# Feeding x to the attention block: split in SBUF and turned by DMA, loaded ahead of Wv, with the opening's slots rearranged

## What is computed

```python
x = x + xattn(_layernorm(x), ctx, Wq, Wk, Wv, Wo)   # 32 heads of 128, 4 key/value groups
x = x + ffn(_layernorm(x), w_gate, w_up, w_down)    # 512 -> 1376 -> 512, quantised weights and activations
# in xattn: keys and values come from concatenate([context, latents]); latents = _layernorm(x)
```

## Time and profile before

| | |
|---|---|
| median of 3 runs | 822.93 us (822.24 to 824.15) |
| the profiled execution's own time | 823.92 us |
| its span in the trace | 822.1 us |
| PE busy | 780.0 us (95%) |
| DVE, ACT, POOL busy | 599.8, 433.7, 229.4 us |

### The profile page before, as it was taken

The page is one execution under the profiler, slowest core; times in us unless marked ns, Lnnn a source line. Parts: engine busy times, 40 slices in busy tenths (PEclk is TensorE's granted clock), DMA queues, the critical chain, the costliest instruction groups (busy, mean ns, idle before and its releaser), DMA issues.

```text
span 822.1 us, 12689 instructions
## 1 busy us (share of the span) xinstructions
PE 780.0 (95%) x4803; PEld 471.6 (57%) x4803; DVE 599.8 (73%) x1117; ACT 433.7 (53%) x940; POOL 229.4 (28%) x366
## 2 busy tenths in 40 slices
PE   8999999999999999999999999998989999941998
PEld 3456576667666666666666666665544444420445
DVE  5876557788767878768778777888767559989431
ACT  6255446655656655656655655555631019782920
POOL 0120314356343355442456433434300000000000
PEclk9999999999999999999999999999999999985999
DMA  9214046757455666455765546888752000000011
GB/s 318 79 61 145 14 90 143 158 137 141 112 120 131 164 154 134 111 129 115 180 137 137 125 102 131 170 164 151 153 98 47 1 1 0 1 0 0 27 39 39
DMA packets 203582, 85.51 MB, mean 104 GB/s; under 512 B 170369, under 2 KB 187009, under 8 KB 203521
## 3 DMA queue, kind: packets, MB, share of 16 engines
q1 hardware_dynamic: 203520, 84.69, 44.8%
HBM read 31.72 MB, written 10.75 MB: 52 GB/s over the span
## 4 chain that ended last, share of the span: by engine, by line
PE 84%; DVE 9%; DMA 3%; POOL 1%; issue 1%; ACT 1%; SPq 1%; DVEq 0%; ACTq 0%; POOLq 0%
PE bank L328 25%; PE bank L446 12%; PE bank L513 12%; PE bank L430 10%; PE bank L418 10%; PE bank L582 7%; PE bank L450 6%; DMA arena<-in_x 2%; DVE arena L769 2%; DMA arena<-arena 1%; DVE stats L1122 1%; DVE arena L1112 1%; POOL arena L1155 1%; DVE bn L924 1%; PE bank L355 1%
## 5 line engine op out<-in xcount | busy, mean ns | idle before, releaser
L328 PE MATMUL bank<-arena 128*128 128x256 f16 (+1 forms) x1872 | 260.6, 292 | 1.7 <-DVE arena L769 1.7
L328 PEld LDWEIGHTS bank<-arena 128*128 128x128 f16 x1872 | 183.0, 98 | 83.2 <-DVE arena L769 3.2
L1155 POOL TENSOR_SCALAR arena<-arena,rsum 128x256 f32<-128x256 f32 x256 | 133.2, 520 | 299.9 <-DVE rsum L835 285.7
L769 DVE SCALAR_TENSOR_TENSOR arena<-bank,arena 128x512 f16<-128x512 f32 x168 | 114.7, 689 | 121.0 <-ACT arena L590 120.8
L590 ACT ACTIVATE arena<-bank 128x512 f16<-128x512 f32 x168 | 98.8, 597 | 179.2 <-PE bank L430 103.1
L769 DVE SCALAR_TENSOR_TENSOR arena<-arena 128x512 f16<-128x512 f32 (+5 forms) x197 | 171.0, 881 | 17.8 <-ACT arena L590 17.2
L590 ACT ACTIVATE arena<-arena 128x512 f16<-128x512 f32 (+5 forms) x164 | 130.1, 819 | 34.5 <-POOL arena L1185 13.1
L632 ACT ACTIVATE arena<-bank,nmax 128x256 f32<-128x256 f32 x256 | 117.7, 471 | 49.0 <-DVE nmax L827 48.7
L446 PE MATMUL bank<-arena 128*128 128x512 f16 x512 | 121.0, 379 | 0.4 <-ACT arena L590 0.4
L513 PE MATMUL bank<-arena 128*128 128x512 f16 x507 | 109.8, 379 | 0.2 <-DVE stats L1053 0.2
L430 PE MATMUL bank<-arena 128*128 128x512 f16 x384 | 94.6, 383 | 4.1 <-DMA arena<-arena 4.1
(11 more groups left out here) (102 smaller groups left out, 496.2 us busy)
## 6 DMA issues: line engine op xcount, KB each, us to landing
arena<-in_w_units SPq DMA_DIRECT2D x33, 256.0 KB, 3.6
w_ready<-arena SPq DMA_DIRECT2D x33, 256.0 KB, 3.3
arena<-in_wq SPq DMA_DIRECT2D x32, 256.0 KB, 3.6
arena<-in_wo SPq DMA_DIRECT2D x32, 256.0 KB, 3.6
arena<-in_x SPq DMA_DIRECT2D x1, 2048.0 KB, 15.2
out<-arena SPq DMA_DIRECT2D x7, 256.0 KB, 2.0
arena<-in_wk SPq DMA_DIRECT2D x4, 256.0 KB, 5.0
arena<-in_ctx_t SPq DMA_DIRECT2D x4, 256.0 KB, 5.2
```

The costliest lines, as they stand in the source:

```text
L328: last = nc.tensor.matmul(bank, a(i, c), b(j, c), start=start and c == 0 and n == 0, stop=stop and c == chunks - 1 and n == 2)
L769: return nc.vector.scalar_tensor_tensor(out=dst, in0=src, scalar=scale, in1=part, op0=ALU.mult, op1=ALU.subtract)
L1155: done = nc.gpsimd.tensor_scalar(p_s[:, t % 2, :, hh, :], p_s[:, t % 2, :, hh, :], rsum[:, t % 2, hh:hh + 1], P_SCALE, ALU.mult, ALU.mult)
```

## The change

x is loaded in two halves, ahead of Wv. The normalised x carries the factor 64 (folded into `veps`), its upper part is written by ACT (`x_upper`, 128 x 512 a batch), its lower part by POOL (a `tensor_tensor` subtraction of 128 x 512 a batch), both into `x_16` in SBUF, and SP turns each batch with one DMA transpose of 128 x 1024 fp16 into `src_t[:, 5]` (`turn_x`). PE's fp32 transposes and the two splits from their banks are gone. DVE takes two `bn_stats` in each of slots 0 to 3, aggregates in slot 3 and splits Wv there; ACT splits Wv's upper part in slot 3. `ln_apply` stands in slots 5 and 6. The second half of the context is split in two pieces of two chunks, and PE multiplies by pairs. The units of the opening begin in slots 8, 11, 15, 25. At slot 16 ACT waits until all eight transposes have landed, because the buffer of `x_16` becomes that of the split Wq.

```diff
-SLOT_OF = (5, 9, 13, 25)
+SLOT_OF = (8, 11, 15, 25)
+        x_16 = f16(96, 8192).rearrange("p (b r n) -> p b r n", b=B, r=2)
 # SP
+            for half in range(2):
+                sp.dma_start(y[:, 4 * half:4 * half + 4, :], x_d[:, 4 * half:4 * half + 4, :]).then_inc(x_loaded[half], 16)
             sp.dma_start(wkv_raw[:, 1], wv_d).then_inc(wv_loaded, 16)
-            sp.dma_start(y, x_d).then_inc(x_loaded, 16)
+            def turn_x(b):
+                sp.wait_ge(x_lo, b + 1)
+                sp.dma_start_transpose(src_t[:, 5, :, :, b * P:(b + 1) * P].rearrange("p r c t -> p (r c) t"),
+                                       x_16[:, b].rearrange("p r n -> p (r n)")).then_inc(x_turned_in[b // 4], 16)
...
             load_unit(0)
+            for b in range(B):
+                turn_x(b)
             for slot in range(32):
 # PE
-            pe.wait_ge(src_lo, HC + 1)
             for g in range(NG):
-                three(banks[4 + g][:, :], lambda r, c: wkv_s[:, 0, r, c, g * D:(g + 1) * D],
-                      lambda r, c: src_t[:, 0, r, c, 512:TOK], HC).then_inc(kv_mm, 1)
+                for pair in range(2):
+                    pe.wait_ge(src_lo, HC + 1 + pair)
+                    mm = three(banks[4 + g][:, :], lambda r, c: wkv_s[:, 0, r, 2 * pair + c, g * D:(g + 1) * D],
+                               lambda r, c: src_t[:, 0, r, 2 * pair + c, 512:TOK], HC // 2, start=pair == 0, stop=pair == 1)
+                mm.then_inc(kv_mm, 1)
             for b in range(B):
                 v_tile(0, (4 if b < 4 else 8) + b + 1, b, b % 4)
-                if b >= 4:
-                    transpose_x(2 * (b - 4))
-                    transpose_x(2 * (b - 4) + 1)
             for i in range(2):
-                pe.wait_ge(xt_free, i * 4 + 8)
+                pe.wait_ge(x_turned_in[i], 64)
 # ACT
-            hi(src_t[:, 0, 0, :, 512:TOK], ctx_raw[:, :, 512:TOK], X_SCALE).then_inc(src_hi, 1)
-            act.wait_ge(wv_loaded, 16)
-            hi(wkv_s[:, 1, 0], wkv_raw[:, 1], W_SCALE).then_inc(wv_hi, 1)
+            for c in range(0, HC, 2):
+                hi(src_t[:, 0, 0, c:c + 2, 512:TOK], ctx_raw[:, c:c + 2, 512:TOK], X_SCALE).then_inc(src_hi, 1)
...
                     k_hi(slot + 1, 0, slot // 4, slot % 4, slot)
+                    if slot == 3:
+                        act.wait_ge(wv_loaded, 16)
+                        hi(wkv_s[:, 1, 0], wkv_raw[:, 1], W_SCALE).then_inc(wv_hi, 1)
+                    if slot == 7:
+                        for b in range(4):
+                            x_upper(b)
                 elif slot < 16:
+                    if slot < 10:
+                        x_upper(2 * slot - 12)
+                        x_upper(2 * slot - 11)
                     v_hi(slot + 1, (slot - 8) * P, slot % 4)
...
                     if slot == 16:
-                        act.wait_ge(wv_lo, 1)
+                        for turned in x_turned_in:
+                            act.wait_ge(turned, 64)
 # DVE
                     k_lo(slot + 1, 0, slot // 4, slot % 4, slot)
+                    if slot < 4:
+                        dve.wait_ge(x_loaded[slot // 2], 16)
+                        nc.vector.bn_stats(bn[:, 2 * slot, :], y[:, 2 * slot, :]).then_inc(ln_stat, 1)
+                        nc.vector.bn_stats(bn[:, 2 * slot + 1, :], y[:, 2 * slot + 1, :]).then_inc(ln_stat, 1)
+                    if slot == 3:
...
+                        nc.vector.tensor_scalar(veps[:, :], mv[:, :, 1], 1e-5, X_SCALE ** -2, ALU.add, ALU.mult).then_inc(ln_var, 1)
+                        dve.wait_ge(wv_hi, 1)
+                        lo(wkv_s[:, 1, 1], wkv_raw[:, 1], wkv_s[:, 1, 0], W_SCALE).then_inc(wv_lo, 1)
+                    if slot == 5:
+                        dve.wait_ge(ln_rstd, 1)
+                    if 5 <= slot < 7:
+                        for b in range(4):
+                            ln_apply(4 * (slot - 5) + b)
 # POOL
-                if slot == 8:
+                if slot == 4:
                     pool.wait_ge(mhalf_set, 1)
                     pool.wait_ge(ln_var, 1)
                     nc.gpsimd.tensor_tensor(rstd[:, :], veps[:, :], mhalf[:, :], ALU.pow).then_inc(ln_rstd, 1)
+                if slot == 8:
+                    for b in range(B):
+                        pool.wait_ge(x_hi, b + 1)
+                        nc.gpsimd.tensor_tensor(x_16[:, b, 1, :], xln[:, b, :], x_16[:, b, 0, :], ALU.subtract).then_inc(x_lo, 1)
```

More of the change, by code:

```diff
@@ L177, in build @@
         wk_loaded = [sem(f"wk_loaded{c}") for c in range(HC)]
-        wv_loaded, x_loaded = sem("wv_loaded"), sem("x_loaded")
+        wv_loaded, x_loaded = sem("wv_loaded"), [sem("x_loaded0"), sem("x_loaded1")]
         wq_loaded = [sem("wq_loaded0"), sem("wq_loaded1")]
@@ L188, in build @@
         kv_mm, kv_hi, kv_free = sem("kv_mm"), sem("kv_hi"), sem("kv_free")
-        xt_mm, xt_hi, xt_free = sem("xt_mm"), sem("xt_hi"), sem("xt_free")
+        x_hi, x_lo, x_turned_in = sem("x_hi"), sem("x_lo"), [sem("x_turned_in0"), sem("x_turned_in1")]
         ln_stat, ln_mv = sem("ln_stat"), sem("ln_mv")
@@ L342, in v_tile @@
                       lambda r, c: wkv_s[:, 1, r, c, :], HC).then_inc(kv_mm, 1)
[L344 to L350, removed]
             def keep_warm(n):
@@ L369, in _ @@
                         mm.then_inc(kv_mm, 1)
-            pe.wait_ge(src_lo, HC + 1)
             for g in range(NG):
-                three(banks[4 + g][:, :], lambda r, c: wkv_s[:, 0, r, c, g * D:(g + 1) * D],
-                      lambda r, c: src_t[:, 0, r, c, 512:TOK], HC).then_inc(kv_mm, 1)
+                for pair in range(2):
[3 more added lines that the diff above has]
+                mm.then_inc(kv_mm, 1)
             pe.wait_ge(wv_lo, 1)
-            pe.wait_ge(ident_set, 2)
             for b in range(B):
                 v_tile(0, (4 if b < 4 else 8) + b + 1, b, b % 4)
-                if b >= 4:
-                    transpose_x(2 * (b - 4))
-                    transpose_x(2 * (b - 4) + 1)
             for i in range(2):
-                pe.wait_ge(xt_free, i * 4 + 8)
+                pe.wait_ge(x_turned_in[i], 64)
                 for g in range(NG):
@@ L454, in transpose_x2 @@
             def transpose_x2(b):
+                if b == 0:
+                    pe.wait_ge(ident_set, 2)
                 pe.wait_ge(ln2_out, b + 1)
@@ L467, in x_value_tile @@
                       lambda r, c: wkv_s[:, 1, r, c, :], HC).then_inc(kv_mm, 1)
-            pe.wait_ge(xt_free, 12)
             for f in range(3):
@@ L613, in v_hi, with x_upper @@
                 hi(kv[:, 1:5, 2, col:col + P], banks[bank][:, :].rearrange("p (g d) -> p g d", g=NG), PROJ_OUT).then_inc(kv_hi, 1)
[L615 to L618, removed]
+            def x_upper(b):
+                if b == 0:
+                    act.wait_ge(wv_lo, 1)
+                act.wait_ge(ln_out, b + 1)
+                hi(x_16[:, b, 0, :], xln[:, b, :], 1.0).then_inc(x_hi, 1)
             def q_upper(f):
@@ L664, in _ @@
                     k_hi(slot + 1, 0, slot // 4, slot % 4, slot)
+                    if slot == 3:
[4 more added lines that the diff above has]
+                            x_upper(b)
                 elif slot < 16:
+                    if slot < 10:
+                        x_upper(2 * slot - 12)
+                        x_upper(2 * slot - 11)
                     v_hi(slot + 1, (slot - 8) * P, slot % 4)
-                    if slot >= 12:
-                        xt_upper(2 * (slot - 12))
-                        xt_upper(2 * (slot - 12) + 1)
                 elif slot < 24:
                     if slot == 16:
-                        act.wait_ge(wv_lo, 1)
+                        for turned in x_turned_in:
+                            act.wait_ge(turned, 64)
                     k_hi(slot + 1, 1, (slot - 16) // 4, slot % 4, slot % 4)
@@ L781, in _ @@
             dve.sem_inc(kv_free, 4)
-            dve.sem_inc(xt_free, 4)
             dve.sem_inc(g_free, 3)
@@ L796, in v_lo @@
                    kv[:, 1:5, 2, col:col + P], PROJ_OUT).then_inc(kv_free, 1)
[L798 to L802, removed]
             def wq_lower(n):
@@ L896, in _, with ln_apply @@
                 lo(src_t[:, 0, 1, c, 0:512], ctx_raw[:, c, 0:512], src_t[:, 0, 0, c, 0:512], X_SCALE).then_inc(src_lo, 1)
[L897 to L900, removed]
-            for slot in range(32):
-                if slot == 8:
[L904 to L912, removed]
+            for c in range(0, HC, 2):
+                dve.wait_ge(src_hi, HC + 1 + c // 2)
+                lo(src_t[:, 0, 1, c:c + 2, 512:TOK], ctx_raw[:, c:c + 2, 512:TOK], src_t[:, 0, 0, c:c + 2, 512:TOK], X_SCALE).then_inc(src_lo, 1)
+            def ln_apply(b):
+                nc.vector.tensor_scalar(xln[:, b, :], y[:, b, :], mv[:, b, 0:1], rstd[:, b:b + 1],
+                                        ALU.subtract, ALU.mult).then_inc(ln_out, 1)
+            for slot in range(32):
                 if slot == 24:
@@ L921, in _ @@
```

(13 more changed lines are left out.)

## The result

The changed kernel takes 817.0 us (median of 4 runs, 816.17 to 817.2) against 823.39 (4 runs, 822.24 to 824.15): a ratio of 0.992, 95% interval 0.9908 to 0.9933, or 6.4 us won. The forecast was 817.8, from a gain of 5.1. Of all executions behind this document two were disturbed (1201.59 us of before and 2277.39 us of a variant) and are in no ratio. The first page part and the windows of the kernel after answer to the earlier trace rows; two windows at the loop's end are added.

The account below looks back on a forecast made before the run. PE bounds the kernel, busy 780.0 of 822.1 us. Removing waits of 0.54 and 1.09 and transposes of 3.51 wins 5.14, so 822.93 - 5.1 = 817.8 us; range 816.9 to 821.2.

Parts of the forecast that it names:

- The opening: PE before x's key tiles: waits of 0.54 and 1.09 and transposes of 3.51 go, together 5.14 us; start at 47.7.
- rival 2: Opening: DVE and POOL hold each other up, costing PE 0 to 0.9 us; gain about 4.2, time 818.7; chance 0.20.
- Context pieces and Wv: Opening: DVE's context pieces end at 15.1 and 16.2, Wv's split at 26.4; PE asks for Wv at 26.90, margin 0.5.
- POOL's power "ends by 26": Opening, ahead of x's normalisation: POOL's power, 1.70 us in the profile, ends by 26, behind Wv's split.
- the 4 us of cover: Fifth value tile: first `v_lo` done by 33.1, PE wants it at 37.3, so the wait of 1.09 goes.
- The rule on the port: Opening: DVE and GpSimd share one port pair, so normalisations (4 x 1.05 = 4.2) and POOL (some 2.7) delay each other.
- DMA transposes: Opening, x's eight transposes on SP: issued 1.35 us apart, last landing 43.2; second unit's load about 44.5, its `v_lo` 46.
- 5.1 us arrive at the end undiminished: After the opening: later unit stages are absorbed by DVE's slack, so the whole 5.1 us gain reaches the end.
- everything there is timed from PE's progress: Queries, scores and loop: they follow PE, so the 5.1 us gain passes through them unchanged.
- The size: Whole kernel: gain 5.1 us, from a median of 822.93 to 817.8; chance 0.52, own range 816.9 to 818.5.

Follow-up runs that it names:

- later stores: The changed kernel with SP's store of each opening unit one slot later, the load of Wq ahead of the third unit's store: 816.3 us, again 815.98.
- old slots: The changed kernel with the units of the opening begun in the slots of before (5, 9, 13, 25): 829.04 us, ratio 1.0065.
- Wv first: The changed kernel with Wv loaded ahead of x again, as in the kernel before: 817.6 us, ratio 0.9925.
- no clash: The changed kernel with POOL's eight subtractions held until DVE has written all eight normalised batches: 819.95 us, ratio 0.9955.
- pieces alone: The kernel before with only the context's second half split in two pieces on ACT, DVE and PE: 823.64 us, ratio 0.9998.

## Why the prediction was right or wrong

- **The opening**: right in the sum, and by 0.1 us of luck in the path (see rival 2 below). 5.14 forecast, 5.07 measured. Key tiles of x start at 47.72 (forecast 47.7), and PE's timeline shows no wait from 6.14 to 73.8.
- **Context pieces and Wv**: right. The rows of after have DVE's pieces at 14.06 to 16.4, Wv's split from 24.22 to 26.51 (26.4); PE asks at 26.93.
- **POOL's power "ends by 26"**: wrong by 2. It begins at 24.47 inside DVE's split of Wv and takes 3.59 instead of 1.70. That took 0.6 of the 4 us of cover at the fifth value tile: the normalisations start at 28.10 (27.5).
- **The rule on the port and rival 2**: the mechanism came, and at the fifth value tile with the rival's own number. The forecast had the first `v_lo` by 33.1, the rival at "about 37.3 or later", against PE at 37.3. It ran from 36.60 to 37.28 (DVE of after, from 37.25 to 37.5):

```profile
36.60 0.68 DVE L777 SCALAR_TENSOR_TENSOR arena<-bank,arena 128x512 f16<-128x512 f32 x1
```

The fifth value tile starts at 37.34, 0.30 after the matmul ahead of it instead of 0.22, so PE lost 0.08: the cover was used up, 0.6 by the power and 3.6 by the normalisations, 7.3 instead of 3.74. That the loss was at the lowest end of the rival's 0 to 0.9 is luck. At the third value tile the `v_lo` was done at 41.85 against 42.5. The subtraction cost 9.88 / 8 = 1.24, under the 1.39 from which PE would feel it, but over the 1.05 taken.
- **DMA transposes**: near. Issued in 10.96, 1.37 each (1.35), last landing 43.4 (43.2); the second unit's load landed at 44.44 (44.5) and its `v_lo` was done at 46.8 (46), against PE at 47.7.
- **"5.1 us arrive at the end undiminished"**: this is the step that failed, in three places. I followed SP's queue to the second unit's load and not on to the third unit's store, behind which the loads of Wq stand: 0.85 lost, 0.74 of it shown by the run with later stores. And "everything there is timed from PE's progress" holds from 77 to 566 us, to 0.01, but not in the last steps, where PE waits for DMA: 4.56 us of waits stood in the trace of before, and I had not asked what sets them. 1.35 of these went, because 72 PE instructions fewer moved the fetches off the last transpose. The clock's fall, which is in half of the runs of before, went with them, 0.7 in the median. The prediction had all three at nothing.
- **The size**: the gain was 6.39 and not 5.14, and above the 6.0 at the end of the forecast's range (822.93 - 816.9). The 1.25 between them are -0.07 in the opening, -0.85 at the query tiles, +1.35 of waits, 0.1 of small distances, and +0.7 of clock. The forecast time looks nearer than that, 0.8, because it started from 822.93 and the median of the comparison is 823.39.

What the cause at the loop's end rests on: five kernels with after's PE program, whose loops begin at different times (after, old slots, Wv first, no clash, later stores), all end with waits of 0.52 to 0.79, 1.19 to 1.72 and 0.42 or 0.43; two with the PE count of before (before, pieces alone), with 1.95 or 1.97 and 2.05 or 2.19; and 184 instructions more take before's last wait to 0.43. So these waits go with PE's instruction count and not with the time. That the fetch is the link is shown by its packets inside the slow transposes, and by the two packets of 4 bytes that it holds back in the last one. Yet 72 more in after do not bring 2.19 back, only 0.80, since there the two packets pass ahead of it. What decides that order, and why only half of the runs of before lose clock behind the wait, stays open.

## What to carry to other kernels

An edit that wins in one stage is to be followed through every later wait of the bound engine, those for transfers at the end of the program too: what sets them may depend on something the edit changes by the way, here the number of instructions. A total that comes out does not show that the margins did: here a cover of 4 us had shrunk to nothing. On an in-order queue follow everything behind a moved transfer to its last reader, not only the next load. And where runs of one kernel fall in two groups, compare groups with the same granted clock before explaining a difference of 1 us.

## What the runs showed of the hardware

- PE's instructions were fetched in packets of 16 KB on q8, one for 256 instructions (255 to 257 between the last six packets of after). In the twelve traces the 638 loop transposes (128 x 2048 fp16, SBUF to SBUF) without such a fetch inside landed after 4.22 to 5.28 us, median 4.26, and the 130 with one after 4.22 to 6.49, median 5.72. In the stretch of before's last transpose the fetch is 0.9% of the DMA time, and that transpose lands after 6.0.
- A granted clock below 1 followed PE standing for 2.19 us in before, for 1.97 and 2.05 with pieces alone, for 2.07 without the clash and for 8.72 with the old slots. None followed 1.95 in before, nor 1.83, 1.79, 1.75 and 1.72 in other runs.
- POOL's power on 128 x 8 took 1.70 us alone and 3.59 beside a DVE split with both inputs in SBUF; its input also differs by the factor folded into `veps`, and no run separates the two. `ln_apply` took 0.48 alone and the subtraction 1.12; beside each other both ran at one in 1.30 (means 1.17 and 1.24 over groups that overlap in part). The Trainium skill, "SBUF — State Buffer", section "Who interferes with whom", describes a shared port pair of these two engines; the trace agrees in direction, in both directions.
- Eight DMA transposes of 128 x 1024 fp16 from SBUF to SBUF were issued every 1.37 us and landed after 3.4, much like those from memory (1.35 and 3.9).
